# A pre-norm attention and feed-forward block: keys stacked in another layout, the split of the attention output moved to VectorE, and the start put in another order

## The reference, cut to what matters

```python
tgt1 = layer_norm(tgt, g1, be1)
q, k, v = (tgt1 @ W.T + b for each of Wq, Wk, Wv)        # 16 heads of 16
score = einsum('bshd,bthd->bhst', q, k) / 4 + (1 - mask) * -1e9
o = einsum('bhst,bthd->bshd', softmax(score), v)
tgt = tgt + o @ Wo.T + bo + memory @ Wg.T + bg
tgt1 = layer_norm(tgt, g2, be2)
out = tgt + relu(tgt1 @ W1.T + b1) @ W2.T + b2
```

## Time and profile before

| | |
|---|---|
| median of three runs | 1938.49 us |
| the profiled execution, its own time | 1938.98 us |
| its span, first to last instruction | 1937.4 us |
| TensorE busy / weight loads | 93% / 90% |
| ScalarE / VectorE / GpSimd busy | 77% / 64% / 43% |
| mean granted clock of TensorE | 0.992 of full speed |

### The profile page before, as it was taken

How to read it: one execution, slowest core, us unless ns; L and a number is a source line. 1 busy time by engine, 2 the same in 40 slices (tenths; PEclk the granted TensorE clock), 3 DMA queues, 4 the chain that set the end, 5 groups by cost and what they waited for, 6 DMA issues and landing times.

```text
span 1937.4 us, 54246 instructions
## 1 busy us (share of the span) xinstructions
PE 1808.3 (93%) x17972; PEld 1743.6 (90%) x17972; DVE 1236.3 (64%) x6745; ACT 1492.5 (77%) x5641; POOL 841.5 (43%) x907
## 2 busy tenths in 40 slices
PE   5799999999999999999999999999999999999997
PEld 4699999999999999999999999999999999999987
DVE  5566666666666666666666666666666666666662
ACT  3787787787787787787787787787787787787782
POOL 2244444444444444444444444444444444444444
PEclk8899999999999999999999999999999999999999
DMA  7765765765765755755756756756756756756740
GB/s 148 93 87 93 111 86 91 113 85 90 115 84 90 112 86 92 110 88 92 110 86 93 110 86 94 109 86 95 110 85 95 107 86 97 105 87 98 100 67 22
DMA packets 222662, 183.69 MB, mean 95 GB/s; under 512 B 14768, under 2 KB 197424, under 8 KB 222384
## 3 DMA queue, kind: packets, MB, share of 16 engines
q1 hardware_dynamic: 222384, 180.23, 63.2%
HBM read 62.73 MB, written 16.78 MB: 41 GB/s over the span
## 4 chain that ended last, share of the span: by engine, by line
PE 58%; ACT 32%; issue 5%; DVE 3%; DMA 1%; SPq 0%; ACTq 0%; POOL 0%; DVEq 0%; POOLq 0%
ACT scores L361 18%; PE ffn_ps L779 8%; PE ffn_ps L781 8%; PE ffn_ps L780 8%; PE turn_ps L842 8%; PE work_ps L779 6%; PE work_ps L781 5%; PE work_ps L780 5%; ACT hid L408 4%; PE value_ps L867 3%; PE score_ps L828 3%; PE work_ps L796 3%; ACT k_hi L434 3%; DVE attnT_lo L564 2%; ACT q_hi L425 2%
## 5 line engine op out<-in xcount | busy, mean ns | idle before, releaser
L361 ACT ACTIVATE scores<-scores,row_min 128x128 f32<-128x128 f32 x2048 | 798.1, 410 | 0.2
L705 POOL TENSOR_TENSOR hT_lo<-hid,hT_hi 128x512 fp32r<-128x512 f32 x256 | 331.1, 1293 | 635.8 <-DVE hT_hi L627 635.8
L371 ACT ACTIVATE probs<-turn_ps 128x512 f32<-128x512 f32 x512 | 307.7, 602 | 309.6 <-PE turn_ps L842 308.2
L599 DVE CUSTOM_DVE_ANT_0 scores<-score_ps,mask_bias 128x128 f32<-128x128 f32 x2048 | 471.5, 286 | 2.9 <-issue 2.7
L361 ACT ACTIVATION_READ_ACCUMULATOR scores<-scores,row_min 128x1 f32 x2048 | 427.8, 209 | 0.0
L842 PE MATMUL turn_ps<-ident,scores 128*128 128x128 f32 x2048 | 310.7, 275 | 2.0 <-ACT probs L371 2.0
L779 PE MATMUL ffn_ps<-zT_hi,w_lo 128*128 128x256 f32 x1024 | 304.7, 298 | 5.6 <-ACT hid L408 4.8
L779 PE MATMUL ffn_ps<-w_hi,hT_lo 128*128 128x256 f32 x1024 | 303.0, 296 | 1.9 <-ACT hid L408 1.9
L781 PE MATMUL ffn_ps<-zT_hi,w_hi 128*128 128x256 f32 x1024 | 290.3, 283 | 0.0
L780 PE MATMUL ffn_ps<-zT_lo,w_hi 128*128 128x256 f32 x1024 | 289.0, 282 | 0.0
L781 PE MATMUL ffn_ps<-w_hi,hT_hi 128*128 128x256 f32 x1024 | 287.4, 281 | 0.0
(11 more groups left out here) (112 smaller groups left out, 4203.7 us busy)
## 6 DMA issues: line engine op xcount, KB each, us to landing
q_stack<-q_hi SPq DMA_DIRECT2D x128, 256.0 KB, 6.9
k_stack<-k_hi SPq DMA_DIRECT2D x256, 128.0 KB, 6.0
x_in<-x_dram SPq DMA_DIRECT2D x64, 256.0 KB, 3.8
mem_in<-memory_dram SPq DMA_DIRECT2D x64, 256.0 KB, 6.7
x_res<-x_dram SPq DMA_DIRECT2D x64, 256.0 KB, 6.9
q_stack<-q_lo SPq DMA_DIRECT2D x64, 256.0 KB, 4.2
k_stack<-k_lo SPq DMA_DIRECT2D x128, 128.0 KB, 5.7
out_dram<-y SPq DMA_DIRECT2D x64, 256.0 KB, 2.1
```

The lines of the kernel that those rows point to most:

```text
L361: last = act.activation(scores[:, k, h, :], scores[:, k, h, :], ACT.Exp, bias=row_min[:, k, h:h + 1], scale=-1.0, accum_out=row_sum[:, k, ...
L371: act.activation(probs[:, k % CPB, :], turn_ps[k % 2][:, :], ACT.Copy).then_inc(probs_copied, 1)
L599: last = dve.tensor_tensor_reduce(out=scores[:, t, h, :], in0=score_ps[t % 2][:, h * S:(h + 1) * S], in1=mask_bias[:, b, :], scale=1.0, sc ...
L705: pool.tensor_tensor(halves[1], src, halves[0], ALU.subtract).then_inc(done, 1)
```

## The change

Four things are changed.

1. `k_stack` has its free dimensions in the order chunk, e, (k and b), s. A DMA of keys now writes one run of 512 numbers (2 KB) for each partition and chunk; the moving operand of the score matmul is two runs of 128 columns that lie 2 KB apart.
2. The high part of the attention output is made by VectorE right behind the product at tick 2, no longer by ScalarE at tick 4. The low part stands at tick 3, no longer at tick 4.
3. At the start GpSimd does the root for group 0 before the zero fills, and fills the second pair of stacks behind the root for group 1. TensorE's wait for zeros moves from before the first turn of x to the first scores of each pair of stacks.
4. At the start VectorE takes the statistics of the first x ahead of the reordering of q's weight columns, and normalises it ahead of q's fold and split. The fold and split of k's weights stand behind the low part of x (tick 1 of iteration -1), those of v's behind k_lo (tick 6). TensorE's small product of v's weights with be1 moves behind the product of the keys.

```diff
-        k_stack = [sb(f"k_stack{n}", [P, CPB, KT * GB, 2, S], F32R) for n in range(2)]
+        k_stack = [sb(f"k_stack{n}", [P, CPB, 2, KT * GB, S], F32R) for n in range(2)]
...
-                        sp.wait_ge(zeros_set, 4)
+                        sp.wait_ge(zeros_set, 2 * g + 2)
...
-                            sp.dma_start(k_stack[g % 2][to:to + HD, :, :, e, :]
-                                         .rearrange("p r k s -> p (r k) s").bitcast(F32),
-                                         kk[high_low][HALF * e:HALF * (e + 1)]
-                                         .rearrange("p k (b s) -> p (k b) s", b=GB).bitcast(F32)
+                            sp.dma_start(k_stack[g % 2][to:to + HD, :, e].bitcast(F32),
+                                         kk[high_low][HALF * e:HALF * (e + 1)].bitcast(F32)
                                          ).then_inc(k_stacked, 16)
...
-                    if out_ and t == 4:
-                        g = i - 1
-                        split_high(attn[:], attnT[0], attn_ready, g + 1, proj_ready,
-                                   g if later(g) else None, attnT_hi)
...
                         dve.tensor_tensor(attn[:], value_tiles, inv[:], ALU.mult).then_inc(attn_ready, 1)
+                        dve.wait_ge(attn_ready, g + 1)
+                        if later(g):
+                            dve.wait_ge(proj_ready, g)
+                        dve.tensor_copy(attnT[0][:], attn[:]).then_inc(attnT_hi, 1)
...
-                    if is_at(i, -1) and t == 3:
+                    if is_at(i, -1) and t == 1:
+                        fold_and_split("k")
+                        dve.wait_ge(shift_added, 2)
+                    if is_at(i, -1) and t == 6:
+                        fold_and_split("v")
                         dve.wait_ge(shift_added, 3)
-                    if out_ and t == 4:
+                    if out_ and t == 3:
                         split_low(attn[:], attnT, attnT_hi, i, attnT_split)
...
-                    if is_at(i, -2) and t == 10:
-
+                    if is_at(i, -2) and t == 6:
+                        set_columns("q")
+                    if norm and t == 10:
+                        layer_norm_apply(i + 2, x_in, mv1, rstd1, ln1_rstd, xhat, x_turned, ln1_ready)
+                    if is_at(i, -2) and t == 11:
                         set_columns("k")
                         fold_and_split("q")
-                    if norm and t == 10:
-                        layer_norm_apply(i + 2, x_in, mv1, rstd1, ln1_rstd, xhat, x_turned, ln1_ready)
-
-            set_columns("q")
-            run(dve, iteration, after_first=keys_and_values, after_second=low_parts)
+
+            run(dve, iteration, after_second=low_parts)
...
-            for n in range(2):
+            def set_zeros(n):
+                pool.wait_ge(ln1_rstd, n + 1)
...
-            run(pool, iteration)
+            run(pool, iteration, after_first=lambda: set_zeros(0), after_second=lambda: set_zeros(1))
...
                     if c == 0:
+                        if i < 2:
+                            pe.wait_ge(zeros_set, 2 * i + 2)
                         pe.wait_ge(q_stacked, 16 * TERMS * (i + 1))
...
-                                     k_stack[i % 2][:, c, GB * k + b].rearrange("p e s -> p (e s)"),
+                                     k_stack[i % 2][:, c, :, GB * k + b, :],
...
+                        if is_at(i, -1) and which == 1:
+                            shift_product("v")
...
-            for name in "qkv":
+            for name in "qk":
                 shift_product(name)
             pe.wait_ge(ident_loaded, 16)
-            pe.wait_ge(zeros_set, 4)
```

More of the change, by code:

```diff
@@ L505, in fold_and_split @@
                 low_part(name)
-            def keys_and_values():
-                fold_and_split("k")
-                fold_and_split("v")
             def low_parts():
@@ L677, in _ @@
                 pool.wait_ge(zeros_set, 2 * n + 1)
-                pool.memset(k_stack[n][:].rearrange("p r k e s -> p (r k e s)").bitcast(F32), 0.0
+                pool.memset(k_stack[n][:].rearrange("p r e k s -> p (r e k s)").bitcast(F32), 0.0
                             ).then_inc(zeros_set, 1)
```

## The result

| | before | after |
|---|---|---|
| median | 1938.62 us (4 runs) | 1845.56 us (4 runs, 1842.75 to 1845.98) |
| ratio, 95% interval | | 0.9516 [0.9499, 0.9532] |
| profiled execution: own time, span | 1938.98, 1937.4 | 1845.47, 1843.8 |

The forecast was 1842 in a range from 1834 to 1880. The total is 3.6 us off. Two of its terms were off by more, 4 and 8 us, with opposite signs, so part of that closeness is luck.

A forecast was written before the change was run, and what follows sets the result against it. The prediction took TensorE's wait for attnT_lo, caused by the order of instructions on ScalarE, to bound the steady part. 1938.98 - 96 (wait) - 1 (start), with zero for the key layout, gave 1842 us, range 1834 to 1880.

The forecast's parts named there:

- The wait: TensorE's projection waits for attnT_lo, 1.53 us in each of 63 iterations; the reorder removes it, gaining 96 us, at least 81.
- the third up product: TensorE's wait for ScalarE's relu (hid), 8.3 us in all, binding 8 times in 63, should stay as it was.
- The other signs: Matmuls busy 97 or 98% of the span, first scores within 35 to 42 us, mean of the score matmuls unchanged.
- the fall of 73,728 packets: Key copies in 2 KB pieces: packets under 2 KB were to fall by 73,728.
- The block of the cast: VectorE's new high-part cast waits for GpSimd's memT_hi, ending at 1034.2, within 1.97 us of idle time.
- In the steady part that is worth nothing: Faster key copies, some 5.5 us a group and not 8, gain nothing, as TensorE waits for keys only at the start.
- The layout at the start: Keys land sooner, 5.5 in place of 8 us, but a gain also needs the chain through w2's low part.
- The slower rival: Two runs of the moving operand slow the score matmuls; at half speed 123 us more, 1965; chance 0.03.
- The start: Reordered normalisation, fills and weight splits before the first scores: 5 us gained at best, 1.5 lost at worst, 1 taken.
- The sum: Whole kernel: 1938.98 less 96 for the wait and 1 for the start, giving 1842 us.

The follow-up runs named there:

- the two experiments on the place in the lists: Kernel before with the attention output's high part one place earlier on ScalarE: 1864.63 us; or on VectorE but late, at tick 4: 1894.49 us.
- the attention part alone: Kernel before with VectorE making the attention output's high part behind the product at tick 2, low part at tick 3, old key layout: 1887.26 us, ratio 0.9736.
- the two kernels with the second fills moved: Second fills behind v's split: in the changed kernel, 1839.78 us; with attention part, key layout and the old start, 1837.56 us.

## Why the prediction was right or wrong

**The wait: right.** 1.53 us per iteration were forecast for the kernel as changed, and 1.59 measured, 27.55 us against "near 27.6". No wait took its place there, the third up product stayed where it was (8.3 us both times), and the two experiments on the place in the lists confirm that the order was what cost: on ScalarE by its time (0.9593), on VectorE by the 49.6 us of wait that a late place left. The other signs came as well: matmuls busy for 97%, first scores at 39.66 us, the mean of a score matmul 284 ns in both kernels. One was misnamed: the fall of 73,728 packets is that of all packets (222,662 to 148,934); those under 2 KB fell by 98,304, since the new pieces of 2 KB are not under 2 KB.

**The block of the cast: right.** I let it wait for `memT_hi` and end 1034.2 - 1032.74 = 1.46 us after `attn`. It ended 1015.32 - 1014.04 = 1.28 us after `attn`, and the idle time took it in. The Trainium skill's rule (SBUF — State Buffer, "Who interferes with whom") I had called unshown for a subtraction with two SBUF inputs. Two rows show it now, from both sides: 1.68 us for GpSimd's `hT_lo` when VectorE was first, 1.23 for VectorE's `attnT_lo` when GpSimd was.

**"In the steady part that is worth nothing": wrong.** This is the step that failed on the key layout. The old layout does cost nothing in an iteration of 29.15 us. In one of 27.55 it costs 28.28 - 27.55 = 0.73 us each, 46 us in all (49 by the times of the two kernels), so that half of the gain I gave to the attention part alone belongs to the two parts together. The sentence before it, that the q copies go out 0.8 us later and are "needed some 16 us on", held the error: I called 16 us plenty without adding up what has to be done in them. With the old layout the way from the q copies to the first scores took 16.3 us, where TensorE came to them after 15.8. An estimate could have been made from the earlier trace rows: 768 KB at 147 GB/s and 768 KB at 97 GB/s are 5.4 + 8.1 = 13.5 us, which leaves 2.5 of the 16 for issue and landing. The forecast came right because the change did both. That was luck: the layout had a price of nothing in it.

The Trainium skill's sentence that copies from SBUF to SBUF don't suffer from small pieces (DMA: Bandwidth & Descriptors, "Why small descriptors are slow (HBM only)") doesn't hold for this kernel: the same bytes of keys in 512-byte pieces held the pipeline up by 49 us. From issue to landing a copy of k_hi took 8.1 us in the attention part alone and 7.0 with the layout (medians). What it is in a small piece that costs isn't shown.

**The layout at the start: wrong by 1.5 to 5 us.** I had it at no gain of its own. The key layout alone is that much faster, nearly all of it in the first groups, and part of it may be the granted clock.

**The slower rival: wrong.** Two runs of columns have the same 280 ns.

**The start: wrong.** Forecast was a gain of 1 us with 5 and -1.5 as ends. The new start costs 7.3 us. The block of v's fold was foreseen (27.6 for v's low part; 30.26 came). Not foreseen were two things. The first fill blocked the first normalisation, 5.57 us, so that x's low part came at 15.77 and not 13: I had applied the rule to q's bias, which stood there before, and not to what the change put in its place. And the 3.63 us of w1's shift became 6.82. Its windows (stretch, length, busy by engine, PEclk), before and after:

```profile
27.90:31.50 3.60, 3.60 (x34) 3.55 (x32) 1.47 (x5) 0.00 (x0) 0.00 (x0) 1.00 1.10 121
```

```profile
33.00:39.60 6.60, 6.60 (x34) 6.60 (x32) 1.47 (x5) 0.00 (x0) 0.00 (x0) 0.50 0.60 87
```

The same 32 products, at a granted clock of 1.00 (2.4 GHz) before and of 0.50 (1.2 GHz) after. Ahead of v's product TensorE had waited 7.8 us after the change. That wait isn't the whole cause: in the two kernels with the second fills moved the shift ran at 0.50 as well (6.82 us of matmuls in both), though the wait was 4.0 us in the one, and in the other 2.2, as in the kernel before, with v's product at 1.00. What lowered the clock is open. The 3.2 us are a part of the 7.3, and of what the moved fills didn't bring back.

**The sum.** 96 + 1 forecast, 93 measured: attention part and layout together gave 100 (1938.31 - 1838.15) where I had 96, and the new start took 7 where I had it giving 1.

What is open: what lowered the clock in w1's shift, how much of the layout's own gain at the start is the clock, and what it is in pieces of 512 bytes that costs.

## What to carry to other kernels

A wait of one engine for a chain over three is a matter of where each link stands in its engine's list; moving one link by one place gave 79 us here without a change in any engine's work. Before calling a hidden cost worthless, shorten the iteration to what you forecast and add its loop up again: transfers that fitted into 29.1 us held the shorter one at 28.3. And when a rule says that two instructions block each other, apply it to every instruction that the new order puts beside the other, not to the one that stood there in the old trace.

## What the runs showed of the hardware

- A GpSimd fill stopped VectorE's TENSOR_SCALAR instructions from SBUF to SBUF until its very end: 5.57, 5.04 and 3.25 us for work of 0.2 to 0.7 us. Not every instruction was stopped: BATCH_NORM_STATS2, which reads x in SBUF, took 0.72 us beside a fill (kernel before, 6.62 us) and 0.74 without one. An addition with one operand in PSUM (v's shift, 128x256) took 0.41 us beside a fill and 0.42 without one.
- A VectorE subtraction of two SBUF operands and one of GpSimd held each other up, by 0.4 to 0.55 us, the later one losing.
- A matmul whose 256 moving columns are two runs 2 KB apart takes as long as with one run (median 280 ns in 1024).
- 32 products with one moving column, each with a weight load of 128 columns, took 3.63 us at the upper clock and 6.82 at the lower: the clock counted although nearly all of the work was weight loads.
